# A tower of nine stages on one core: normalization put into the load blocks, layer 1's pipeline written out, and experts computed under a gather

## What is computed

```python
h = _L0_tok_ref(x, ...)
h = h + _L0_attn_ref(_layernorm(h), ...)
h = h + _L0_ffn_ref(_layernorm(h), ...)
h = h + _L1_attn_ref(_layernorm(h), ...)     # 16 query heads, one key head, window of 128
h = h + _L1_ffn_ref(_layernorm(h), ...)
h = h + _L2_attn_ref(_layernorm(h), ...)
h = h + _L2_ffn_ref(_layernorm(h), ...)
h = h + _L3_attn_ref(_layernorm(h), ...)     # normalizes its input once more inside
h = h + _L3_ffn_ref(_layernorm(h), ...)

def _L3_ffn_ref(x, ...):                     # graph attention routes, 4 experts compute
    agg = segment_sum(h_gat[src] * alpha, dst) + b_gat      # over 262144 edges and the loops
    scores = _layernorm(agg, ln_gamma, ln_beta) ...mean over the heads
    w = softmax(top 2 of scores)
    for ei in range(4):
        g = weight of expert ei, or 0
        hh = gelu(x @ W1[ei] + b1[ei])
        out = out + g * (hh @ W2[ei] + b2[ei])
```

## Time and profile before

| | us |
|---|---|
| median of 3 runs (18895.28 to 18918.06) | 18901.33 |
| the profiled execution | 18988.5 |
| its span, first to last instruction | 18986.7 |
| PE busy | 11533.1 |
| DVE busy | 8751.2 |
| ScalarE busy | 5823.9 |
| POOL busy | 2169.1 |

### The profile page before, as it was taken

How to read it: one execution, slowest core, us unless ns; L and a number is a source line. 1 busy time by engine, 2 the same in 40 slices (tenths; PEclk the granted TensorE clock), 3 DMA queues, 4 the chain that set the end, 5 groups by cost and what they waited for, 6 DMA issues and landing times. The chain is left out here.

```text
span 18986.7 us, 169231 instructions
## 1 busy us (share of the span) xinstructions
PE 11533.1 (61%) x41513; PEld 7179.7 (38%) x41513; DVE 8751.2 (46%) x29125; ACT 5823.9 (31%) x13473; POOL 2169.1 (11%) x2242
## 2 busy tenths in 40 slices
PE   2588599998553311139999999999889610000004
PEld 1477466665323300014444444444567500000004
DVE  5544544444312278876666666666422382111102
ACT  1344234443113310025555555555333200000001
POOL 0000000000000000000000000000000007777771
PEclk5566577777656655569999999999755555555555
DMA  0000000000021100014333444334100104222220
GB/s 3 3 0 0 1 4 0 0 0 2 20 88 44 46 6 2 2 42 98 98 98 98 99 99 98 96 98 99 34 0 0 18 0 43 24 20 20 20 15 10
DMA packets 481191, 688.04 MB, mean 36 GB/s; under 512 B 168462, under 2 KB 423015, under 8 KB 460898
## 3 DMA queue, kind: packets, MB, share of 16 engines
q1 hardware_dynamic: 405826, 641.72, 13.6%
q0 software_dynamic: 74592, 38.28, 3.4%
HBM read 405.88 MB, written 83.41 MB: 26 GB/s over the span
## 5 line engine op out<-in xcount | busy, mean ns | idle before, releaser
L1562 PE MATMUL pm_out<-pm_w,pm_tab 128*128 128x484 f32 x8192 | 4009.8, 570 | 0.2 <-DVE pm_w L1727 0.2
L1727 DVE SCALAR_TENSOR_TENSOR pm_w<-pm_sums,pm_e 128x484 f32<-128x484 f32 x4096 | 2647.2, 658 | 1021.2 <-ACT pm_e L1655 977.8
L1655 ACT ACTIVATE pm_e<-pm_sums 128x484 f32<-128x484 f32 x4096 | 2315.7, 573 | 1407.8 <-PE pm_sums L1576 1406.1
L2292 POOL DMA_INDIRECT g_got<-gat_sources,ed_idx x2048 | 1982.8, 968 | 685.7 <-issue 674.5
L1562 PEld LDWEIGHTS pm_out<-pm_w,pm_tab 128*128 128x128 f32 x8192 | 1555.7, 191 | 1039.7 <-DVE pm_w L1727 593.3
L2208 POOL DMA_INDIRECT ed_first<-gat_targets,so_at x1 | 2.9, 2882 | 15674.2 <-DVE so_at L2218 15674.2
L2450 PE MATMUL g_ps<-k_ident,g_wide 128*20 128x128 f32 x3 | 0.8, 409 | 2885.2 <-DVE g_wide L2472 2885.2
L1576 PE MATMUL pm_sums<-pm_mv,pm_pick 96*128 96x484 bf16 x4096 | 1512.9, 370 | 35.9 <-DMA pm_mv<-pm_parts 20.1
L2450 PEld LDWEIGHTS g_ps<-k_ident,g_wide 128*20 128x20 f32 x3 | 0.3, 111 | 2885.5 <-DVE g_wide L2472 2885.4
L2388 DVE TENSOR_TENSOR g_e<-g_got,g_b 128x512 f32<-128x512 f32 x16 | 11.1, 692 | 2039.4 <-DMA g_got<-gat_sources,ed_idx 2039.3
L2327 ACT ACTIVATE g_ex<-g_ex 128x1024 f32<-128x1024 f32 x16 | 16.9, 1056 | 2795.2 <-DVE g_ex L2403 2795.2
(11 more groups left out here) (496 smaller groups left out, 21224.3 us busy)
## 6 DMA issues: line engine op xcount, KB each, us to landing
pm_tab<-in_L_ffn_tables SPq DMA_DIRECT2D x128, 2048.0 KB, 7.7
pm_mv<-pm_parts SPq DMA_DIRECT2D x3072, 60.5 KB, 2.4
qkv_rows<-p_q SPq DMA_DIRECT2D x32, 1452.0 KB
a_qkv<-qkv_rows SPq DMA_DIRECT2D x96, 484.0 KB
g_got<-gat_sources,ed_idx POOLq DMA_INDIRECT x2048, 2.6
pm_gb<-pk_threshold_rows SPq DMA_DIRECT2D x128, 242.0 KB, 7.2
gat_running<-g_rec SPq DMA_DIRECT2D x16, 1536.0 KB, 5.9
gat_heads<-ed_same SPq DMA_DIRECT2D x4, 1024.0 KB
```

Source lines behind the costliest of these rows:

```text
L1562: pe.matmul(out[:, hd % 2, 0:CHUNK], tab[hd % 2][:, t, :], w[:, t % NW, :], start=(t == 0), stop=(t == KT - 1)).then_inc(used, 1)
L1655: a.activation(e[:, t % NW, :], sums[:, t % NB, 0:CHUNK], ACT.Exp).then_inc(exp_ready, 1)
L1727: v.scalar_tensor_tensor(out=w[:, t % NW, :], in0=sums[:, t % NB, 0:CHUNK], scalar=0.0, in1=e[:, t % NW, :], op0=ALU.is_gt, op1=ALU.mult). ...
L2292: g.indirect_dma_start(got[c][:, w, :], None, rows, bass.IndirectOffsetOnAxis(ap=idx[:, i * W + w:i * W + w + 1].bitcast(U32), axis=0)).th ...
```

## The change

There are three parts.

1. `layernorm_all` is gone. A class `Norm` holds the steps, and `load_all` takes them in its own block: DVE runs them behind its presets, while SP issues the loads. The rows are cut into four quarters of tiles: DVE subtracts the mean in three quarters, POOL in the fourth; ScalarE squares quarter by quarter; DVE reduces each quarter; in the end DVE scales three quarters and POOL the fourth. Semaphores are shared by all normalizations and counted on. The second norm of the third attention is a block without loads and then the block with them.

2. In layer 1's attention the loop is replaced by Python's: all 16 pairs of samples are written out and every wait is for a constant. On PE the wait for the last copy of v (`v3`) stands before the blend at n=4, no longer before the projection at n=0, and the turn of the next sample waits for the `v3` of the sample before.

3. The experts' products don't wait for the gates: PE, ScalarE and DVE compute them inside the block of the gathers, one pair of samples per chunk, ahead of the chunk's own work, and SP stores them in DRAM (`expert_rows`). Their weights are loaded in a block before the gathers. The ring `got` has 3 slots. The block of the gates loads the products in four pieces and weighs, sums and adds them; the block `f3_` is gone.

```diff
-def layernorm_all(nc, h, xn, name):
...
+class Norm:
+    STEPS, ROOTS = 8, 5
+    QUARTERS = [slice(q * TILES // 4, (q + 1) * TILES // 4) for q in range(4)]
...
+    def vector(self, v):
+        v.tensor_reduce(mean, h[:, :, :], AX.X, ALU.add).then_inc(done, 1)
+        v.wait_ge(done, D + 1)
+        v.tensor_scalar(mean, mean, 1.0 / C, None, ALU.mult).then_inc(done, 1)
+        v.wait_ge(done, D + 2)
+        for q in self.QUARTERS[0:3]:
+            v.tensor_tensor(xn[:, q, :], h[:, q, :], spread(mean[:, q], C), ALU.subtract).then_inc(done, 1)
+        for n, q in enumerate(self.QUARTERS):
+            v.wait_ge(self.root, R + n + 1)
+            ins = v.tensor_reduce(var[:, q], sq[:, q, :], AX.X, ALU.add)
+        ins.then_inc(done, 1)
...
+        for q in self.QUARTERS[0:3]:
+            v.tensor_tensor(xn[:, q, :], xn[:, q, :], spread(self.rstd[:, q], C), ALU.mult)
+
+    def gpsimd(self, g):
+        g.wait_ge(self.done, self.D + 2)
+        g.tensor_tensor(xn[:, last, :], h[:, last, :], spread(self.mean[:, last], C), ALU.subtract).then_inc(self.pooled, 1)
+        g.wait_ge(self.done, self.D + 8)
+        g.tensor_tensor(xn[:, last, :], xn[:, last, :], spread(self.rstd[:, last], C), ALU.mult)
+
+    def scalar(self, a):
+        for n, q in enumerate(self.QUARTERS):
...
+            a.activation(self.sq[:, q, :], self.xn[:, q, :], ACT.Square).then_inc(self.root, 1)
+        a.wait_ge(self.done, self.D + 7)
+        a.activation(self.std, self.var, ACT.Sqrt).then_inc(self.root, 1)
...
         def samples(eng, first, body, end):
             first()
-            body(0, True, False)
-            with eng.Fori(1, PAIRS - 1) as i:
-                body(i, False, False)
-            body(PAIRS - 1, False, True)
+            for i in range(PAIRS):
+                body(i, i == 0, i == PAIRS - 1)
             end(PAIRS * 2 * NH)
...
                     if name == "turn":
                         pe.wait_ge(DV, pd.after(b, "x"))
+                        if b:
+                            pe.wait_ge(AC, pa.after(b - 1, "v3"))
...
-                            if n == 0:
-                                pe.wait_ge(AC, pa.after(b, "v3"))
                             project(u, n, c)
                             if not (lead and n < 1):
                                 score(*ago(1))
+                            if n == 4:
+                                pe.wait_ge(AC, pa.after(b, "v3"))
...
-            W, SLOTS, RING = 128, 4, 4
+            W, SLOTS, RING = 128, 3, 4
...
+                            for l in both:
+                                v.wait_ge(mlp[l], ml.before(i))
+                                v.tensor_copy(xs[l][:, :, :], xn[:, (i * LANES + l) * NT:(i * LANES + l + 1) * NT, :]).then_inc(mlp[l], 1)
+                            for l in both:
+                                v.wait_ge(mlp[l], made(i, "y"))
+                                v.tensor_tensor(y[l][:, :, :], ps[l][0:TP, 3, :].rearrange("p (t n) -> p t n", t=NT), repeat(b2[:, :], NT),
+                                                ALU.add).then_inc(mlp[l], 1)
...
+                            if i < CHUNKS:
+                                for c in both:
+                                    sp.wait_ge(mlp[c], made(i, "bias"))
+                                    sp.dma_start(expert_rows[:, (i * LANES + c) * NT:(i * LANES + c + 1) * NT, :], y[c][:, :, :]).then_inc(mlp[c], 16)
...
+                    for q in range(PIECES):
+                        tiles = slice(q * PIECE, (q + 1) * PIECE)
+                        v.wait_ge(y_loaded[q], 16)
+                        v.wait_ge(s, after("gates"))
+                        tt(y[q][:, :, :, :], y[q][:, :, :, :], spread(gates[:, tiles, :], C), ALU.mult).then_inc(s, 1)
+                        v.wait_ge(s, after(f"weigh{q}"))
+                        red(red_[q % 2][:, :, :], y[q][:, :, :, :].rearrange("p t e c -> p t c e"), AX.X, ALU.add).then_inc(s, 1)
+                        v.wait_ge(s, after(f"blend{q}"))
+                        tt(h[:, tiles, :], h[:, tiles, :], red_[q % 2][:, :, :], ALU.add).then_inc(s, 1)
```

More of the change, by code:

```diff
@@ L98, in layernorm_all, with load_all @@
+def load_all(nc, ctx, name, pairs, ones=(), norm=None):
+    sem = ctx.enter_context(nc.semaphore(name + "_preset_and_loaded")) if pairs else None
+    with ExitStack() as own:
+        if norm:
+            norm, h, xn = norm
+            norm.begin(nc, own, name, h, xn)
         with nc.Block() as block:
@@ L250, in stage_l0_attn @@
             (mask[:, :, :], k["strict"]), (valid[:, :], k["valid"])],
[L251 removed]
+            [(xT[c][C:CA, :], 1.0) for c in range(LANES)], norm=(k["norm"], h, xn))
         ident = k["ident"]
@@ L2244, in stage_l3_ffn @@
                 two = range(2)
+                CA, HD = C + 1, 2 * C
+                w1, w2, b2 = sb("w1", [CA, NE, HD]), sb("w2", [HD, NE, C]), sb("b2", [TP, NE * C])
+                xs = [sb(f"xs{c}", [TP, NT, C]) for c in both]
+                xT = [sb(f"xT{c}", [CA, T]) for c in both]
+                hid = [sb(f"hid{c}", [HD, NE, T]) for c in both]
+                y = [sb(f"y{c}", [TP, NT, NE * C]) for c in both]
+                ps = [ctx.enter_context(nc.psum_tensor(f"g3_ps{c}", [128, 4, BANK], F32)) for c in both]
+                load_all(nc, ctx, "f3", [
+                    (w1[0:C, :, :], A["L3_ffn_W1"].rearrange("e c n -> c e n")),
+                    (w1[C:CA, :, :].rearrange("p e n -> p (e n)"), row(A["L3_ffn_b1"].rearrange("e n -> (e n)"))),
+                    (w2[:, :, :], A["L3_ffn_W2"].rearrange("e n c -> n e c")),
+                    (b2[:, :], row(A["L3_ffn_b2"].rearrange("e c -> (e c)")).to_broadcast([TP, NE * C]))],
+                    [(xT[c][C:CA, :], 1.0) for c in both])
+                ml = Chain([ctx.enter_context(nc.semaphore(f"g3_mlp_step{c}")) for c in both], ["x", "turn", "xT", "hid", "gelu", "y", "bias", "store:16"])
+                mlp, made = ml.sem, ml.after
                 got = [sb(f"got{c}", [128, W, SRC]) for c in range(SLOTS)]
@@ L2324, in _ @@
                         for i in range(CHUNKS):
+                            for c in both:
+                                a.wait_ge(mlp[c], made(i, "turn"))
+                                for t in range(NT):
+                                    ins = a.activation(xT[c][0:C, t * TP:(t + 1) * TP], ps[c][t * C:(t + 1) * C, 0, 0:TP], ACT.Copy)
+                                ins.then_inc(mlp[c], 1)
+                            for c in both:
+                                a.wait_ge(mlp[c], made(i, "hid"))
+                                a.activation(hid[c][:, :, :].rearrange("p (k n) w -> p k (n w)", k=2), ps[c][:, 1:3, 0:2 * T], ACT.Gelu).then_inc(mlp[c], 1)
                             c = i % 2
@@ L2515, in stage_l3_ffn @@
                      "square", "var_s", "var", "std", "rstd", "unit", "gamma", "beta", "score", "quarter", "compare", "ties", "beats", "rank",
-                     "chosen", "max", "less", "w_exp", "w", "w_sum", "w_inv", "gates"]
+                     "chosen", "max", "less", "w_exp", "w", "w_sum", "w_inv", "gates"] + [f"{n}{q}" for q in range(PIECES) for n in ("weigh", "blend", "add")]
             chain = Chain([ctx.enter_context(nc.semaphore("g6_step"))], names)
```

200 lines of the change are left out of this document (78 added, 122 removed).

## The result

The changed kernel takes 18207.35 us (median of 4 runs, 18206.31 to 18208.47), the kernel before in the same comparison 18898.31 us (18857.29 to 18918.06). The ratio is 0.9637, with a 95% interval from 0.962 to 0.9654: 691 us less. The prediction was 18305 us, with a range from 18190 to 18440. The time lies in the range, 98 us under the point. That is not one error spread thin: two terms are nearly right and one is too small.

What follows compares the result with a forecast made beforehand. PE paced layer 1 at a mean clock of 0.76, POOL's gathers the graph stage; PE idled in the pauses. 67 + 285 + 245 = 597 us off the 18901.3 us median gave 18304, point 18305, range 18190 to 18440.

Steps and rivals of the forecast that it cites:

- The normalization: In the eight pauses: loads beside the normalization steps, one DVE pass fewer; saves 67 us, 101 and 34 at the bounds.
- the hindrance by POOL: In the pauses: DVE held up by POOL's quarters, taken as 3.7 us per normalization, between nothing and 7.4.
- The other price in the prediction: In the pauses: estimate from the Trainium skill, POOL's two quarters cost 4.5 us per normalization, saving 60 us instead of 67.
- The experts: In the gather block: expert work hidden under POOL's gathers, less 55 us blending and 5 us POOL slowdown; saves 245 us.
- Rivals C and D: Gather block: C, experts' chain delays POOL's gathers, 240 us return, 18544 us, 4%; D, slower by stretched POOL instructions, 2%.
- The upper end of the range, 262: Gather and last blocks: the experts' saving was put at 245 us, from 220 to 262.
- Layer 1: Layer 1's attention without a loop: 18 us idle PE at ten back edges gone, the rest clock; saves 285 us.
- The waits at n=9 stay, and so do falls behind them: Layer 1: clock falls at n=9 remain; fifteen, at the seen proportion of five long to four short, cost 176 us.
- The signs that the prediction named for itself: In the changed profile: layer 1 at about 1920 us, clock near 0.9, falls only behind n=9; pauses 22 to 25 us.
- No two neighbouring samples both have the fall at n=9: Layer 1: at most every second sample falls at n=9; fifteen long falls would bring back 297 us, saving 135.
- Rival A: Layer 1: clock stays full because only back edges made the n=9 pattern; 432 us saved instead of 285, 18157 us, 12%.
- 432 and the 135 on the other side: Layer 1's bounds: 432 us saved if thirty samples take 53.26 us, 135 if every second sample falls long.

## Why the prediction was right, and where it was off

**The normalization.** Forecast 67 us, measured 79.9 by the pauses. The mechanism held: loads and presets lie beside DVE's chain, the squares under the reductions. Of the unknown, the hindrance by POOL, I took 3.7 us per normalization; by the stretches it is 2 x (5.20 - 3 x 1.16) = 3.4. The larger part of the 12 us is in the other terms: quarters one behind another take 1.16 us each and not 1.23, and DVE was busy for 189.6 us where my terms make 9 x (17.67 + 3.7) + 7.8 = 200.1. The other price in the prediction, 4.5 us per normalization, was further off: the hindrance was 3.4. My step gave POOL's quarter a price and didn't ask the question behind it, whether the quarter is worth giving away. It isn't.

**The experts.** Forecast 245, measured 253.3. POOL was not slowed at all (I took 5 us), the last block grew by 50.9 us (55; the reduction took 7.08 instead of 8.1). Nothing waited for the ring. Rivals C and D are refuted by the two rows of POOL. The upper end of the range, 262, has no working in the prediction.

**Layer 1.** Forecast 285, measured 333 by the medians of the kernel with its loop, and 435 between the first two traces. The step that failed is "The waits at n=9 stay, and so do falls behind them", with the long ones taken "in the mix seen". The waits stayed (0.96 us, where the loop had 1.00). The falls behind them stayed too, ten of thirty, but every one was short: they cost 16 us, not 147. The signs that the prediction named for itself, about 1920 us and a clock near 0.9, came as 1770 us and 0.96. "No two neighbouring samples both have the fall at n=9" was also false as a rule; here three in a row have it. Rival A was nearer the right mechanism, and the argument against it, that nine falls stood behind n=9 alone, was the error: they stood behind n=9 in a stage with edges, and no long one stands there in the 150 samples without. The table of the four combinations shows the other side: edges without n=9 are almost as cheap as n=9 without edges, though these edges are shorter too.

**The baseline.** 432 and the 135 on the other side were measured in one execution of a stage that differs by some 90 us from one to the next. I put all 87 us between profile and median on the kernel's account as a whole ("by the profile 18391.5, by the runs 18304"). For the most part they belong to layer 1, the term that I was sizing (48 of 57 us between the two traces). Against the medians, the loop's removal is worth 333 us and not 432. So the too small share (285 of 432) and the too dear baseline partly cancelled, and that is luck: by the profile alone the forecast was 18391.5 us, and the profiled execution took 18206.3, 185 less. Of the 98 us by which the point is off, 48 are layer 1, 24 and 22 the other two parts as taken back, and 4 the medians. Some 25 of the 46 of these two parts lie in stages that no part changed, most of all the second attention's half, which takes 1038 to 1051 us in these kernels and 1038 and 1047 in one and the same; they are no measure of the parts.

Open is what makes one fall short and the next long. The same wait of 0.96 us cost nothing, 1.65 or 20.0 us (69.45 + 56.84 - 2 x 53.14), depending on when it came. The runs show that idle places elsewhere in the stage shift the odds, and that a short fall just before an edge goes with a long one behind it, but not why, nor what share the length of an edge's wait has.

## What to carry to other kernels

Where PE runs at the full clock, price an idle place by the clock it puts at risk together with the other idle places of the stage, and test each combination: removing the last one is worth more than its own length (51 us for 30 of waits here), and removing one of two can be worth most of both. When combinations are compared, read the length of each idle place in each of them again: taking one away can shorten the other. Before a stage is sized from one trace, look at whether the runs of the kernel agree: a spread of 61 us beside one of 2 was the sign that this stage draws its time anew. (So it was later with edges alone, 62 us.) And work given to GpSimd beside VectorE's products is not free work: compare the sum of both with VectorE alone.

## What the runs showed that was not expected

- Chips differ in the issue of gathers. On the chip of the second group a gather took 1046 ns on average, against 968 to 970 on the two other chips, in the kernel without table loads as in the others, and the block of the gathers some 205 us longer (3043 us from its first gather to the next block instead of 2838):

```profile
L2360 POOL DMA_INDIRECT g_got<-gat_sources,ed_idx x2048 | 2141.7, 1046 | 710.7 <-issue 694.1 <-POOLq L135 16.5
```

- Work put on DVE in layer 1 (fourteen instructions and their tile) went with a slower later stage whose code hadn't changed. In both kernels with work at the seams the first part of the product-key stage took 1647.6 us instead of 1622.7, and the difference is time at the issue in front of one line of its loop (groups of DVE there, with 1024 elements at the seams and in the changed kernel; the mean of 231 ns against 208 stands in all four kernels of the second chip and is not the difference meant, the idle time is):

```profile
L1396 DVE MAX8 pk_srt<-pk_sim 121x8 f32<-121x64 f32 x3072 | 396.5, 231 | 236.8 <-issue 236.8
```
```profile
L1393 DVE MAX8 pk_srt<-pk_sim 121x8 f32<-121x64 f32 x3072 | 395.6, 208 | 212.1 <-issue 212.1
```

The kernel without table loads ran on the same chip with 1622.8 us, and the one with the loop of two passes showed 212.3 us at the issue there, so it is the program and not the chip. Nor is it the number of instructions: the kernel without table loads has 320 more on DVE in layer 1. What in it, a position of the loop's code perhaps, wasn't tried.
